# A graph network of six edge sweeps: PSUM operands for VectorE and a new order of its steps within a group

## What is computed

```python
# GAT, 8 heads                       (the sweep called gat)
e = leaky_relu(el[src] + er[dst], 0.01)
# TransformerConv, 4 heads, twice    (tconv);   mha is the same without e
rel_t_enc = cos((node_vec[src] - edge_weight)[:, None] * Wt + bt)
e = concat([rel_t_enc, edge_attr]) @ We
alpha = sum(q[dst] * (k[src] + e), -1) / sqrt(32);   values v[src] + e
# GATv2, 8 heads, twice              (gatv2)
e = sum(leaky_relu(xl[src] + xr[dst], 0.2) * att, -1)
# all:  out[dst] += softmax_over_dst(e) * values[src]
```

## Time and profile before

| | us |
|---|---|
| median of 3 runs | 7290.55 (7282.23 to 7300.37) |
| span of the profiled execution | 7290.4 |
| POOL busy | 5179.0 (71%) |
| VectorE (DVE) busy | 4893.6 (67%) |
| TensorE (PE) busy | 4733.5 (65%) |
| ScalarE (ACT) busy | 4079.6 (56%) |

### The profile page before, as it was taken

One profiled execution on the slowest core, in us unless ns is written; L12 is line 12 of the kernel. 1 busy time (PEld: TensorE's weight loads), 2 busy tenths in 40 slices (PEclk: granted clock), 3 DMA queues, 4 the chain that ended last, 5 costly groups with the idle time before them and its releaser, 6 DMA issues. The chain is left out here.

```text
span 7290.4 us, 132506 instructions
## 1 busy us (share of the span) xinstructions
PE 4733.5 (65%) x30647; PEld 4262.1 (58%) x30647; DVE 4893.6 (67%) x9144; ACT 4079.6 (56%) x9739; POOL 5179.0 (71%) x5105
## 2 busy tenths in 40 slices
PE   2777776577777567777746666645666654666663
PEld 2677775466767457777635565535555553555553
DVE  5777886467777557777655555546777765777776
ACT  1555554466766457667623333326767654767672
POOL 4777774377777577777657777757777766777774
PEclk6777787788888778888868778867888876888886
DMA  2677775289998578898847777735555553555553
GB/s 71 183 192 194 194 196 157 69 251 258 259 261 256 154 219 258 255 261 255 228 116 208 206 203 206 206 102 148 159 159 159 159 139 97 159 159 159 159 159 88
DMA packets 1717674, 1334.47 MB, mean 183 GB/s; under 512 B 384948, under 2 KB 1559891, under 8 KB 1717524
## 3 DMA queue, kind: packets, MB, share of 16 engines
q1 hardware_dynamic: 1516788, 837.31, 40.0%
q0 software_dynamic: 200736, 495.45, 24.8%
HBM read 913.26 MB, written 418.79 MB: 183 GB/s over the span
## 5 line engine op out<-in xcount | busy, mean ns | idle before, releaser
L739 POOL DMA_INDIRECT s_rows<-kv_tab,s_idx x2352 | 2359.8, 1003 | 737.3 <-issue 703.8
L739 POOL DMA_INDIRECT s_rows<-xl_tab,s_idx x1568 | 1622.5, 1035 | 491.6 <-issue 476.8
L902 PE MATMUL bank<-s_qwin,s_hot_t 128*128 128x128 f32 (+1 forms) x9408 | 1657.2, 342 | 12.9 <-ACT s_hot_t L766 7.1
L928 PE MATMUL bank<-s_msg,s_hot 128*128 128x144 f32 (+1 forms) x9408 | 1553.5, 313 | 126.1 <-ACT s_part L810 90.9
L902 PEld LDWEIGHTS bank<-s_qwin,s_hot_t 128*128 128x128 f32 x9408 | 1557.9, 256 | 57.0 <-issue 31.0
L928 PEld LDWEIGHTS bank<-s_msg,s_hot 128*128 128x128 f32 x9408 | 1351.1, 211 | 189.0 <-ACT s_part L810 145.1
L917 PE MATMUL bank<-ident,s_alpha 128*32 128x128 f32 (+1 forms) x588 | 182.6, 310 | 1512.8 <-DVE s_alpha L1042 1506.1
L810 ACT ACTIVATE s_part<-bank 128x288 f32<-128x288 f32 (+1 forms) x2352 | 901.2, 403 | 352.5 <-PE bank L928 299.7
L917 PEld LDWEIGHTS bank<-ident,s_alpha 128*32 128x32 f32 (+1 forms) x588 | 62.6, 107 | 1598.6 <-issue 1598.4
L780 ACT ACTIVATE s_gap<-iota_free,rank_col 128x128 bf16<-128x128 f32 x3136 | 989.5, 387 | 0.1
L798 ACT ACTIVATE s_prob<-s_diff 32x128 f32<-32x128 f32 (+1 forms) x588 | 180.3, 307 | 1436.2 <-DVE s_diff L997 1407.5
(11 more groups left out here) (292 smaller groups left out, 6193.9 us busy)
## 6 DMA issues: line engine op xcount, KB each, us to landing
s_qwin<-q_tab SPq DMA_DIRECT2D x3920, 64.0 KB
part_tab<-s_part SPq DMA_DIRECT2D x294, 576.0 KB
part_tab<-s_part SPq DMA_DIRECT2D x294, 544.0 KB
s_attr_t<-attr_tab SPq DMA_DIRECT2D x196, 512.0 KB
attr_tab<-s_attr_t SPq DMA_DIRECT2D x98, 512.0 KB
s_rows<-kv_tab,s_idx POOLq DMA_INDIRECT x2352
s_rows<-xl_tab,s_idx POOLq DMA_INDIRECT x1568
s_attr<-in_edge_attr SPq DMA_DIRECT2D x97, 256.0 KB
```

The source lines that it names most:

```text
L739: pool.indirect_dma_start(out=rows[u][:, t, :], out_offset=None, in_=tab, in_offset=bass.IndirectOffsetOnAxis(ap=idx[u][:, t:t + 1], axis= ...
L902: ins = pe.matmul(q_ps[h][:, (t - h * per) * QW:(t - h * per + 1) * QW], hot_t[:, t, :], qwin[u][:, t, :], start=True, stop=True)
L928: ins = pe.matmul(part_ps[c % 2][:, t * W:(t + 1) * W], hot[u][:, PAIR * c + t, :], msg[:, PAIR * c + t, :], start=True, stop=True)
```

## The change

- `messages` reads the probabilities and maxima in PSUM, where `turn_probs` leaves them. `copy_probs` and `pm` go. `turn_alpha(n)` now waits for `messages(n-1)`, and `messages` for `turn_probs`. `msg` has two buffers.
- The constants `iota_free`, `Wt`, `bt` and `att` are copied once a sweep into PSUM bank 4, and L981, L1052, L1054 and L1037 read them there. `fwd` of `maxima` lies in PSUM, and so does the angle in gat.
- L1036, the leaky slope of gatv2, stays as it was.
- VectorE's body: in tconv and mha `messages(n-1)` stands between the two halves of `scores(n)`. In gatv2 both additions come ahead of it, and the rest of both halves (`weigh`) after it. In gat the order is angles, messages, scores.
- In gat the one-hot becomes bfloat16 with a cast on ScalarE, as in the other sweeps, L1061 goes and ScalarE takes the absolute value (`folds`), and the transposes of the edge attributes use one PSUM bank in two turns.

```diff
-        pm = sb("pm", [P, 2 * R])
-        msg = sb("msg", [P, G, W])
+        msg = [sb(f"msg{u}", [P, G, W]) for u in range(2)]
...
-        hot_ps = [pl.banks[0], pl.banks[2]] if kind == "gat" else [pl.banks[0][:, :].bitcast(BF16)]
+        hot_ps = pl.banks[0][:, :].bitcast(BF16)
         q_ps = [pl.banks[1], pl.banks[2]]
         e_ps = [pl.banks[3], pl.banks[4]]
+        if kind == "gat":
+            ang_ps, turn_ps = pl.banks[2], pl.banks[3]
+        const = pl.banks[4]
+        iota_ps, Wt_ps, bt_ps, att_ps = const[:, 0:P], const[:, P:P + 64], const[:, P + 64:2 * P], const[:, P:2 * P]
         small = pl.banks[5]
         alpha_t = small[0:R, 0:P]
+        fwd = small[0:R, 3 * P:4 * P]
         prob_ps, max_ps = small[:, P:P + R], small[:, P + R:P + 2 * R]
...
-                def copy_probs(i, k, u, n):
-                    wait(act, prob_turned, i + 1)
-                    if n >= 1:
-                        wait(act, msg_done, 3 * i)
-                    act.activation(pm[:, :], small[:, P:P + 2 * R], ACT.Copy).then_inc(prob_copied, 1)
...
+                def folds(i, k, u, n):
+                    wait(act, angle_done, i + 1)
+                    act.activation(ang2[u][:, :, :], ang2[u][:, :, :], ACT.Abs).then_inc(folded, 1)
...
                 def turn_alpha(i, k, u, n):
                     wait(pe, alpha_done, QB * (i + 1))
                     if n >= 1:
-                        wait(pe, prob_copied, i)
+                        wait(pe, msg_done, 3 * i)
...
                         ins = pe.matmul(part_ps[c % 2][:, t * W:(t + 1) * W], hot[u][:, PAIR * c + t, :],
-                                        msg[:, PAIR * c + t, :], start=True, stop=True)
+                                        msg[u % 2][:, PAIR * c + t, :], start=True, stop=True)
...
-                    out = hot[u] if kind == "gat" else hot_b[u % 2]
-                    v.tensor_tensor(out[:, :, :], bc(pl.iota_free[:, :].unsqueeze(1), [P, G, P]),
+                    v.tensor_tensor(hot_b[u % 2][:, :, :], bc(iota_ps.unsqueeze(1), [P, G, P]),
                                     bc(pl.rank_col[:, bass.ds(i * G, G)].unsqueeze(2), [P, G, P]),
                                     ALU.is_equal).then_inc(hot_built, 1)
...
+                def scores(i, k, u, n, h):
+                    if h == 0:
+                        wait(v, gathered[u], 16 * G * (k + 1))
+                        if n >= 1:
+                            wait(v, alpha_turned, i)
+                    wait(v, q_done, 2 * i + h + 1)
+                    t0, t1 = h * HALF, (h + 1) * HALF
+                    q = q_ps[h][:, :].rearrange("p (t d) -> p t d", t=HALF)
+                    if kind == "tconv":
+                        e = e_ps[h][:, :].rearrange("p (t d) -> p t d", t=HALF)
+                        kv = rows[u][:, t0:t1, :].rearrange("p t (a d) -> p t a d", a=2)
+                        v.tensor_tensor(kv, kv, bc(e.unsqueeze(2), [P, HALF, 2, D]), ALU.add).then_inc(e_used, 1)
+                        wait(v, e_used, 2 * i + h + 1)
+                    if kind == "gatv2":
+                        v.tensor_tensor(prod[h][:, :, :], q, rows[u][:, t0:t1, :], ALU.add).then_inc(q_used, 1)
+                    else:
+                        v.tensor_tensor(prod[h][:, :, :], q, rows[u][:, t0:t1, 0:D], ALU.mult).then_inc(q_used, 1)
+                        wait(v, q_used, 2 * i + h + 1)
                         v.tensor_reduce(alpha[:, t0:t1, :], prod[h][:, :, :].rearrange("p t (h c) -> p t h c", c=C),
                                         AX.X, ALU.add).then_inc(alpha_done, 1)
 
+                def weigh(i, k, u, n, h):
+                    then = stepper(i, h)
+                    wait(v, q_used, 2 * i + h + 1)
+                    t0, t1 = h * HALF, (h + 1) * HALF
+                    flat = prod[h][:, :, :].rearrange("p t d -> p (t d)")
+                    v.scalar_tensor_tensor(flat, flat, 0.2, flat, ALU.mult, ALU.max).then_inc(leaked, 1)
+                    wait(v, leaked, 2 * i + h + 1)
+                    then(v.tensor_tensor(prod[h][:, :, :], prod[h][:, :, :], bc(att_ps.unsqueeze(1), [P, HALF, D]), ALU.mult))
+                    v.tensor_reduce(alpha[:, t0:t1, :], prod[h][:, :, :].rearrange("p t (h c) -> p t h c", c=C),
+                                    AX.X, ALU.add).then_inc(alpha_done, 1)
...
-                    a, tn = ang[:, :, :].rearrange(fl), turns[:, :, :].rearrange(fl)
+                    a, tn = ang_ps[:, :], turns[:, :, :].rearrange(fl)
+                    a3 = a.rearrange("p (t c) -> p t c", t=G)
...
-                    then(v.scalar_tensor_tensor(a, tn, -TWO_PI_LOW, a, ALU.mult, ALU.add))
                     if n >= S:
                         wait(v, cos_done, i - S + 1)
-                    v.scalar_tensor_tensor(ang2[u][:, :, :].rearrange(fl), a, -1.0, a, ALU.mult, ALU.min
+                    v.scalar_tensor_tensor(ang2[u][:, :, :].rearrange(fl), tn, -TWO_PI_LOW, a, ALU.mult, ALU.add
                                            ).then_inc(angle_done, 1)
...
                 def messages(i, k, u, n):
-                    wait(v, prob_copied, i + 1)
-                    if n >= 1:
-                        wait(v, part_done, NPAIR * i)
+                    out = msg[u % 2]
+                    wait(v, prob_turned, i + 1)
+                    if n >= 2:
+                        wait(v, part_done, NPAIR * (i - 1))
                     vals = rows[u][:, :, TW - D:TW] if kind in ("tconv", "mha") else rows[u][:, :, 0:D]
-                    p = pm[:, 0:R].rearrange("p (t h) -> p t h", h=H)
-                    v.tensor_copy(msg[:, :, D:D + H], p).then_inc(msg_done, 1)
-                    v.tensor_tensor(msg[:, :, 0:D].rearrange("p t (h c) -> p t h c", c=C),
+                    p = prob_ps.rearrange("p (t h) -> p t h", h=H)
+                    v.tensor_copy(out[:, :, D:D + H], p).then_inc(msg_done, 1)
+                    v.tensor_tensor(out[:, :, 0:D].rearrange("p t (h c) -> p t h c", c=C),
                                     vals.rearrange("p t (h c) -> p t h c", c=C),
                                     bc(p.unsqueeze(3), [P, G, H, C]), ALU.mult).then_inc(msg_done, 1)
 
-                    v.tensor_tensor(msg[:, :, D + H:W], pm[:, R:2 * R].rearrange("p (t h) -> p t h", h=H),
+                    v.tensor_tensor(out[:, :, D + H:W], max_ps.rearrange("p (t h) -> p t h", h=H),
                                     bc(pl.last_col[:, bass.ds(i * G, G)].unsqueeze(2), [P, G, H]), ALU.mult
                                     ).then_inc(msg_done, 1)
 
...
                     if has(n, -1):
                         maxima(*near(*g, -1))
-                    if has(n):
-                        scores(*g)
                     if kind == "gat":
                         if has(n):
                             angles(*g)
                         if n == NG - 1:
                             v.wait_ge(attr_turned, 2 * (NG - S))
                             v.memset(attr[(NG - 1) % S][:, :, 64:D], 0.0).then_inc(tail_zeroed, 1)
-                    if has(n, -1):
-                        messages(*near(*g, -1))
+                        if has(n, -1):
+                            messages(*near(*g, -1))
+                        if has(n):
+                            scores_gat(*g)
+                    else:
+                        if has(n):
+                            scores(*g, 0)
+                            if kind == "gatv2":
+                                scores(*g, 1)
+                        if has(n, -1):
+                            messages(*near(*g, -1))
+                        if has(n):
+                            if kind == "gatv2":
+                                weigh(*g, 0)
+                                weigh(*g, 1)
+                            else:
+                                scores(*g, 1)
                     if not act_builds and has(n, 2):
                         build_hot(*near(*g, 2))
 
+                if not act_builds:
+                    ins = v.tensor_copy(iota_ps, pl.iota_free[:, :])
+                    if kind == "gat":
+                        v.tensor_copy(Wt_ps, w["Wt"][:, :])
+                        ins = v.tensor_copy(bt_ps, w["bt"][:, :])
+                    ins.then_inc(const_ready, 1)
+                    v.wait_ge(const_ready, 1)
+                if kind == "gatv2":
+                    v.tensor_copy(att_ps, w["att"][:, :]).then_inc(const_ready, 1)
+                    v.wait_ge(const_ready, 1)
```

More of the change, by code:

```diff
@@ L570, in edge_sweep @@
         hot = [sb(f"hot{u}", [P, G, P]) for u in range(S)]
-        if kind != "gat":
-            hot_b = [sb(f"hot_b{u}", [P, G, P], BF16) for u in range(2)]
+        hot_b = [sb(f"hot_b{u}", [P, G, P], BF16) for u in range(2)]
         if act_builds:
@@ L626, in edge_sweep @@
         step = sem("score_step")
-        STEPS = {"gat": 7, "gatv2": 4}.get(kind, 0)
+        STEPS = {"gat": 6, "gatv2": 2}.get(kind, 0)
         if kind in ("gat", "tconv"):
@@ L839, in body @@
```

(27 more changed lines are left out.)

96 lines of the change are left out of this document (28 added, 68 removed).

## The result

The changed kernel takes **7766.5 us** (7761.6 to 7768.5, 4 runs) against 7287.1 us of the kernel before, a ratio of 1.0653 [1.0638, 1.0668]. Forecast was 7748 us, range 7340 to 7930. The profiled execution has a span of 7759.8 us, 469.4 more than before.

A forecast was written before the change was run, and what follows sets the result against it. The sweeps were taken as gather-bound on POOL, 10.0 us a group at its floor. 7290.4 + 280 (tconv ring) + 272 (gatv2 ring) - 94 (stretched gathers) = 7748 us, range 7340 to 7930.

The forecast's parts named there:

- gat: gat sweep: its stretched gathers go while POOL still bounds, up to 62 us, of which 45 us were taken.
- mha: mha sweep: its stretched gathers go and POOL keeps the bound, so the sweep falls by 49 us.
- tconv ring: tconv: TensorE 7.46 us plus VectorE's steps and handovers give 11.86 us a group, 1.43 more; +280 us for two sweeps.
- gatv2 ring: gatv2: TensorE 6.0 us plus 6.1 us on VectorE give 12.1 us a group against 10.71; +272 us for two sweeps.
- The ring: Closed chain from turn_alpha through turn_probs on TensorE, messages and later scores on VectorE, to the next turn_alpha; nothing overlaps.
- TensorE's stretch in tconv: L917's start to L910's end: 5.83 us at full clock, taken as 7.46 us after about 3 us idle.
- gatv2's stretch: TensorE's part in gatv2: 3.93 us at full clock, taken as 6.0, mean of 5.7 and 6.4, with 4.9 us idle.
- Stretched gathers: POOL's gathers held up by VectorE instructions with two SBUF operands; PSUM operands end this, -94 us in gat and mha.
- rival (4): Gathers stay stretched although operands move to PSUM, and the ring binds all the same: 7842 us, 8%.
- The slope in gatv2: L1036 in gatv2 still reads its tile twice and would keep about half of the 70 us of stretched gathers.
- Rival (2): TensorE at full clock in both tconv (10.23 us) and gatv2 (10.03 us a group): faster, 7024 us, 7%.
- Rival (3): The ring does not bind because turn_probs is done early; all excess goes but half of gatv2's: 7025 us, 3%.

The follow-up runs named there:

- old order: Changed kernel with VectorE's order of before in tconv and gatv2, operands still in PSUM: 7064.5 us, 0.9691 of the kernel before.
- The kernel with TensorE kept busy: Changed kernel plus 8 (tconv) or 14 (gatv2) unused matmuls a group ahead of turn_alpha: 6990.6 us, 0.9594 of the kernel before.
- the two kernels with a shorter ring or no ring: Changed kernel with turn_probs ahead of turn_hot and two sum_parts on TensorE, 7057.2 us; changed kernel with VectorE's earlier order in tconv and gatv2, 7064.5 us.

## Why the prediction was right

The sign and the mechanism came out as forecast, and the size nearly so; that the total is within 12 us is in part luck, as the steps show:

| step | forecast | measured |
|---|---|---|
| gat | -45 us | -49 |
| mha | -49 | -47 |
| tconv ring, per group | 11.86 us | 12.30 and 12.25 |
| tconv, both sweeps | +280 | +358 |
| gatv2 ring, per group | 12.1 | 11.91 and 11.93 |
| gatv2, both sweeps | +272 | +230 |
| outside | 0 | -22 |
| span | 7748 | 7759.8 |

- **The ring.** Its VectorE half was right to 0.04 us in tconv: 4.40 forecast, 4.36 measured (12.30 - 7.94). In gatv2 6.1 was forecast and 5.92 measured, because the two `weigh` follow each other in 4.17 us (5509.39 to 5513.56), not 4.32, and the handovers are short.
- **TensorE's stretch in tconv** is the term that was mis-sized. I had two rows after 3 us of idle, 7.5 and 8.4 us, and took the shorter with the reason that "now and then such a group still runs at 5.8". None did: the shortest of both sweeps was 6.12, the mean 7.92, close to the mean of the two rows (7.95). There are no lucky groups in the ring. That is 0.45 us x 194 = some 80 us too little.
- **The mean of all such rows would not have done much better.** In the trace of the kernel before 20 tconv groups inside the sweeps follow 2.75 to 3.06 us of idle time. Their stretches are 5.7 to 8.6 us with a mean of 7.6, two of them under 6. In the ring, after the same idle time, they are mostly near 7.1, 7.4, 8.2 and 8.8, with a mean of 7.92. So the idle time alone does not set the clock of a stretch; why the ring settles on these values no run shows.
- **gatv2's stretch** of 6.0, the mean of its two rows, was measured at 5.99. This is luck in part: the 26 gatv2 groups before with 4.3 to 5.0 us of idle time took 6.1 to 6.8 us, 6.3 in the mean, and the ring alternates between 5.46 and 6.56. The prediction also rounded this ring up: its parts add up to 12.06 and +265 us, not 12.1 and +272.
- **The errors cancel:** +78 in tconv, -42 in gatv2, -2 in gat and mha, -22 outside the stretches leave 12 us. The total is closer than its terms, and that is luck. The -22 lies at the ends of the sweeps: from the last `turn_alpha` of each to the next sweep's first gather, or to the end, the changed kernel takes 2 to 8 us less. Why stays open.
- **Stretched gathers.** POOL's busy time above 784 x 0.946 us, summed over the six sweeps, fell from 336 to 16 us, and rival (4) is out. The gain could only be cashed where POOL bounds: 96 us in gat and mha. In the old order it is 211 us of the six sweeps. The Trainium skill, "SBUF — State Buffer", section "Who interferes with whom", infers that a tensor_tensor with two SBUF inputs leaves descriptor generation alone. The traces disagree: 96 gathers of the first gatv2 sweep before end 0.81 to 0.83 us behind an L1071, and none does so in the changed kernel. Whether such a gather waits with its read of the indices or with its writing no run shows, so this speaks of these indirect gathers and of no other DMA.
- **The slope in gatv2** was to keep half of the 70 us. It keeps 21 where the gathers bound (old order) and 8 to 9 in the changed kernel.
- **Rival (2)**, full clock in both, had 7024 us and a chance of 7%. The kernel with TensorE kept busy comes within 34 us of its sum (6990.6 us) once the condition is forced; it did not come by itself. Rival (3)'s 7025 is what the two kernels with a shorter ring or no ring come near to (7057 and 7064).
- **Signs that came as written:** VectorE's wait for rows gone and L1073 waiting for L909; gathers at 0.95 us; the clock in gatv2 at 0.78, under 0.81. **One that did not:** POOL was to stand idle for `msg_done`. It stands idle for ScalarE's index copies (800 us against 51 for L1078); they are the last step of ScalarE's body and so come with the ring as late as everything else.

## What to carry to other kernels

When a step is moved on one in-order engine, write out the closed chain from one group's step to the same step of the next, with the other engines' whole queues between the two points, and compare its length with what bounds now; a gain in the bounding resource is lost where such a ring is longer. Count TensorE's part at the clock that it has after the idle time which the ring itself makes: take all groups of the trace that had such an idle time, not the best of two, and leave room, for a steady ring can settle above or below their mean (here 7.9 against 7.6 us, and 6.0 against 6.3). A long ring can be mended on the engine whose order was left alone: one step put ahead on TensorE turned +6.6% into -3.2%.

## What the runs showed of the hardware

- Work without use made the kernel faster. 8 or 14 extra matmuls a group kept the granted clock at 0.99 instead of 0.78 over the tconv and gatv2 sweeps, and 7767 us became 6991. Over the first tconv and the first gatv2 sweep:

```profile
1392.90:2379.10 986.20, 837.50 (x7157) 781.47 (x7158) 730.56 (x1149) 700.70 (x1642) 741.35 (x784) 0.99 0.90 265
...
4772.40:5754.60 982.20, 812.28 (x6808) 754.03 (x6809) 754.93 (x1353) 697.17 (x1648) 743.57 (x784) 0.99 0.60 168
```

  In tconv TensorE, with 1500 more matmul records, was busy 838 us, less than the 869 of the changed kernel.
- The low clock and the ring feed each other: the slower stretch does not shorten VectorE's 4.4 us, in which TensorE stands still again. In no group of the four sweeps did the clock recover by itself. Some of the rhythms are steady for many groups (gatv2: 11.4 and 12.5 us in turn, with stretches of 5.46 and 6.56 us).
- A gather that begins while VectorE runs an instruction with two operands in SBUF ends 0.81 to 0.83 us behind that instruction, instead of 0.95 us after its own start (gathers begun in the last 0.16 us of one came out at their own length). This holds for all 288 stretched gathers of the first gatv2 sweep before (188 at the slope L1036, 96 at L1071, 4 at L1037) and for all 89 of the old order (L1041). In the changed kernel, where these sweeps have one of the two in PSUM, no gather of tconv and mha took over 0.990 us.
- Three chips added idle time, often about 10 and up to 42 us, ahead of single instructions and took a kernel of 7290 us to 10,000; on these the order of the variants was another one.
